# One lane of an attention stage moved one step back in the order that all engines follow

## The reference: what is computed

```python
h = L0_tok(x)                              # 8 x 748 tokens from here on
h = h + L0_attn(layernorm(h))              # a recurrence
h = h + L0_ffn(layernorm(h))               # 8 experts, top 2, and a shared part
h = h + L1_attn(layernorm(h))              # linear attention, below
h = h + L1_ffn(layernorm(h))               # router, 10 experts, shared 9-tap convolution

def L1_attn(x):                            # 8 heads of 16, causal
    q, k, v = split(x @ W_qkv + b_qkv)
    q, k = relu(q), relu(k)
    for w in (cos, sin):                   # position weights
        kv_cum = cumsum(outer(k * w, v));  k_cum = cumsum(k * w)
        ctx += (q * w) @ kv_cum;           nrm += (q * w) . k_cum
    return (ctx / (nrm + 1e-6)) @ W_out + b_out

def L1_ffn(x):
    logits = conv3(gelu(conv3(x, rc_w1)), rc_w2)          # router: 10 scores a token
    experts = top-2 mixture of elu(x @ e_w1) @ e_w2
    shared = conv1(silu(conv9(x, sh_w1)), sh_w2)          # 128 -> 512 -> 128
    return layernorm(x + experts + shared) * ln_g + ln_b
```

## Time and profile before

| | |
|---|---|
| median of 3 runs | 1550.25 us (1546.04 to 1556.02) |
| profiled execution, its own time | 1544.97 us |
| its span, first to last instruction | 1543.1 us |
| PE busy | 1312.4 us, 85% |
| DVE, POOL, ACT busy | 989.1, 698.2, 640.2 us |
| mean granted clock of TensorE | 0.917 |
| attention stage, from the first norm5T on PE to the last rc2 | about 565 to 1178 us |

### The profile page before, as it was taken

The page is one execution under the profiler, slowest core; times in us unless marked ns, Lnnn a source line. Parts: engine busy times, 40 slices in busy tenths (PEclk is TensorE's granted clock), DMA queues, the critical chain, the costliest instruction groups (busy, mean ns, idle before and its releaser), DMA issues.

```text
span 1543.1 us, 33563 instructions
## 1 busy us (share of the span) xinstructions
PE 1312.4 (85%) x10456; PEld 1129.8 (73%) x10457; DVE 989.1 (64%) x3229; ACT 640.2 (41%) x1594; POOL 698.2 (45%) x1055
## 2 busy tenths in 40 slices
PE   5687685976999927798999889988999989999974
PEld 3475654654999915596788778876888989999952
DVE  5386868664566547737762776357752729989956
ACT  2427355331222204245334533435434346666623
POOL 0123645435788833033612353232522536777732
PEclk9798887998999958979998999989998999999987
DMA  6000400003788730100110001000100237777725
GB/s 194 0 21 24 106 20 20 23 19 115 239 257 261 230 109 1 43 1 1 42 43 2 1 22 63 0 2 4 39 1 1 95 104 192 195 195 199 196 88 161
DMA packets 102203, 128.48 MB, mean 83 GB/s; under 512 B 21015, under 2 KB 61181, under 8 KB 101842
## 3 DMA queue, kind: packets, MB, share of 16 engines
q1 hardware_dynamic: 88786, 102.36, 23.0%
q0 software_dynamic: 13312, 24.74, 4.8%
HBM read 96.13 MB, written 34.94 MB: 85 GB/s over the span
## 4 chain that ended last, share of the span: by engine, by line
PE 60%; DVE 16%; issue 7%; DVEq 6%; POOL 4%; ACT 4%; DMA 2%; POOLq 0%; SPq 0%; ACTq 0%
PE psum L977 12%; PE psum L1123 10%; PE psum L986 9%; DVE work L1540 3%; PE psum L1044 3%; PE psum L1102 3%; POOL rows_in L2110 2%; PE psum L1132 2%; PE psum L791 2%; PE psum L1091 2%; PE psum L1069 2%; PE psum L1181 2%; PE psum L966 2%; DVE stats L1523 2%; PE psum L1015 2%
## 5 line engine op out<-in xcount | busy, mean ns | idle before, releaser
L1123 PE MATMUL psum<-NT,wreg 128*128 128x182 f32 (+1 forms) x1536 | 269.6, 333 | 5.2 <-ACT conv_rows L1434 4.3
L1123 PEld LDWEIGHTS psum<-NT,wreg 128*128 128x128 f32 x1536 | 256.2, 197 | 9.9 <-ACT conv_rows L1434 5.4
L2142 POOL DMA_INDIRECT rows_out<-work,expert_row_kept x208 | 206.6, 993 | 78.6 <-issue 40.9
L977 PE MATMUL psum<-work 128*128 128x128 f32 x1664 | 222.8, 277 | 0.9 <-ACT work L1326 0.9
L977 PEld LDWEIGHTS psum<-work 128*128 128x128 f32 x1664 | 204.1, 193 | 1.7 <-issue 0.9
L2091 POOL TENSOR_TENSOR rstd<-var_eps,pack 128x6 f32<-128x6 f32 x40 | 56.7, 1418 | 207.0 <-DVE var_eps L1530 206.7
L1319 ACT ACTIVATE work<-psum,work 128x128 f32<-128x128 f32 x416 | 118.9, 369 | 64.3 <-PE psum L977 64.3
L791 PE MATMUL psum<-pack,work 128*128 128x128 f32 (+2 forms) x288 | 54.0, 348 | 82.5 <-DVE work L1540 75.9
L1862 DVE SCALAR_TENSOR_TENSOR work<-psum,work 128x128 f32<-128x128 f32 x416 | 117.2, 344 | 7.8
L1871 DVE TENSOR_SCALAR work<-psum,expert_row_kept 128x128 f32<-128x128 f32 x208 | 72.8, 350 | 72.1 <-PE psum L966 37.3
L2110 POOL DMA_INDIRECT rows_in<-N,slot_now x96 | 100.6, 1048 | 28.5 <-issue 28.4
(11 more groups left out here) (357 smaller groups left out, 2910.2 us busy)
## 6 DMA issues: line engine op xcount, KB each, us to landing
work<-w_and_b SPq DMA_DIRECT2D x104, 258.0 KB
work<-in_ew SPq DMA_DIRECT2D x104, 256.0 KB
work<-rows_in SPq DMA_DIRECT2D x208, 65.0 KB
work<-rows_out SPq DMA_DIRECT2D x32, 384.0 KB, 4.5
rows_out<-work,expert_row_kept POOLq DMA_INDIRECT x208
work<-in_xT SPq DMA_DIRECT2D x8, 375.0 KB, 4.3
w_and_b<-in_ew SPq DMA_DIRECT2D x1, 2560.0 KB
out<-H SPq DMA_DIRECT2D x8, 320.0 KB
```

What stands on the lines that cost most here:

```text
L977: r_ = mm(v.ps1[:, c * P:(c + 1) * P], v.w1[:, c * P:(c + 1) * P], v.xT, start=True, stop=True)
L1123: r = mm(bank[:, half * HALF_PAIRS:half * HALF_PAIRS + p1 - p0], weights[:, m * P:(m + 1) * P], product_input(name, g, k, p0, p1), start=( ...
L2142: G.indirect_dma_start(rows_out[m], bass.IndirectOffsetOnAxis(ap=v.dest, axis=0), v.y, None, bounds_check=last, oob_is_err=False).then_inc ...
```

## The change

The pairs are now listed with lane 1 one step behind lane 0: step n of lane 0 is followed by step n-1 of lane 1. The list begins with steps 0 and 1 of lane 0 and ends with step 23 of lane 1. The weight of a step in `FILL` goes with the step, so the conv parts shift against the steps a little; the routing work stays tied to its (step, lane). POOL's and SP's lists are not touched.

The DVE work of steps 0 to 2 is handed out anew. Before, it ran as `h3`(0), `var5`(0), `h3`(1), `norm5`(0), `var5`(1), `norm5`(1) (lane in brackets); the new functions give the same row in the new order of steps, and only the convolution's work between them moves.

```diff
         def interleaved(conv):

             order, n, reached = [], 0, 0
-            for x in range(ATT_STEPS * LANES):
-                order.append(("attention", x // LANES, x % LANES))
-                reached += FILL[x // LANES]
+            for x in range((ATT_STEPS + LANES - 1) * LANES):
+                lane_ = x % LANES
+                step = x // LANES - lane_
+                if not 0 <= step < ATT_STEPS:
+                    continue
+                order.append(("attention", step, lane_))
+                reached += FILL[step]
                 while conv and n * sum(FILL) * LANES < reached * len(PARTS) and n < len(PARTS):
                     order.append(("conv", n, 0))
                     n += 1
...
             def begin_lane(k, i):
                 add_experts(k, i)
-                if k == 0:
-                    var5(k, i)
+                if k > 0:
+                    norm5(k - 1, i)
+                var5(k, i)

             def second_step(k, i):
-                (norm5 if k == 0 else var5)(k, i)
-
-            def third_step(k, i):
-                if k > 0:
+                if k == LANES - 1:
                     norm5(k, i)

-            att = {0: [begin_lane], 1: [second_step], 2: [third_step]}
+            att = {0: [begin_lane], 1: [second_step]}
```

## The result

The changed kernel takes 1580.74 us (median of 4 runs, 1574.50 to 1581.97) where the kernel before takes 1548.14 (4 runs, 1545.39 to 1556.02): a ratio of 1.0187, 95% interval 1.0151 to 1.0224. So it is slower by about 1.6%, 21 to 29 us by the ratios. (All ratios here are the recorded ones; the quotients of the medians are 1.0211 and 1.0146.) The profiled execution took 1579.63 us, 34.7 more than that of before.

The account below looks back on a forecast made before the run. PE (TensorE), busy 157.6 of 171.5 us in iteration 2, was taken to set the pace. Terms of 6.3 us an iteration, three times, gave +18.9 us on 1550.25: 1569 us, range 1546 to 1583.

Parts of the forecast that it names:

- norm6T of lane 0: Loop, behind lane 1's last context step: PE waits 3.4 us for DVE's late norm6, +3.2 us an iteration, bounds 2.5 and 4.
- The clock behind it: Behind that new hole TensorE runs 3.4 us at clock 0.50: +1.7 us an iteration, bounds 0 and 3.4.
- rc2 of lane 1: One conv part left between rc1 and rc2; ACT's table load and gelu end late: +0.4 us an iteration, bounds 0 and 0.5.
- Where the chunks begin: First chunks: POOL's `b_v` and `b_sh2` block DVE's first lane 0 state update for 5.9 us; +2.0 us an iteration.
- the wash rival: DVE slips between POOL's instructions and the new hole brings no low clock: 1549 to 1564 us, middle 1556; chance 0.31.
- Where an iteration begins: Iteration start: the hole moves from ahead of q0 to behind it; 0 us, bounds -2 and +1.3.
- rc2's low clock: Around both rc2, now further apart: the 13.7 us at clock 0.50 may break up; -1 us an iteration, bounds -3 and 0.
- The loop's sum: All terms of one loop iteration add to 6.3 us, three times: +18.9 us.
- Iteration 0: Iteration without convolution: gains a q step at its start, loses at its end behind norm6T; 0 us, bounds -4 and +4.
- Much slower: Rival: holes bring two low-clock stretches each and the iteration without convolution loses 4 us; 1583 us, chance 0.06.

Follow-up runs that it names:

- second comparison: The changed kernel measured and profiled again with no edit, against the kernel before: 1573.43 us, ratio 1.0135.
- lag_from_out: Changed kernel with lanes level up to the output projection, lane 1 one step behind only from there on, every iteration: 1566.72 us, ratio 1.0136 to the kernel before.
- level_from_out: Changed kernel with the lag ending at the output projection, lanes level from there on, every iteration: 1558.49 us, ratio 1.0071 to the kernel before.
- changed_mended: Changed kernel with DVE's norm6 of lane 0 ahead of lane 1's last context division, and POOL's conv weights early in iteration 0: ratio 0.9988 to before, on another chip.

## Why the prediction was right, and where it was not

Slower by 18.9 us was forecast; the medians differ by 32.6, and by 22.7 in the second comparison. The total, 1580.7 us, lies in the range of 1546 to 1583, near its end. The direction and the largest term came out by the mechanism that was given. That the total came out no further off is in part luck, since two errors have opposite signs: the loop was forecast 2 to 6 us too long, iteration 0 10 to 15 us too short.

**norm6T of lane 0, +3.2 us.** Right in size (3.65, 3.63 and 3.63 us in the three iterations, against 3.4) and in cause. In the loop the cause is shown three ways: the wait falls to 0.8 us when the context stands ahead of out (`lag_from_out`), and it is gone when the lag ends (`level_from_out`) and when, of the loop's work, DVE's norm6 alone is moved (`changed_mended`).

**The clock behind it, +1.7 us.** Right in place and about right in size. The three low stretches at this hole last 3.4, 6.8 and 3.4 us in the first profile and 6.8, 3.4 and 3.4 in the second. Less the 2.0 and 0.9 us of them that fall into the waits themselves, and halved for the clock, that is an estimated 1.9 to 2.1 us an iteration. They are there whenever the wait is and never without it. What varies between two executions is mostly the low clock elsewhere.

**rc2 of lane 1, +0.4 us.** 0.6 measured.

**Where the chunks begin, +2.0 us.** Wrong. The step that failed is that the first state update of lane 0 would stand still for 5.9 us beside `b_v` and `b_sh2`. It took 0.48 us, and the addition behind it 0.75 beside POOL's 2.24 (iteration 1):

```profile
740.90 0.48 DVE L1938 SCALAR_TENSOR_TENSOR first_row<-pack,psum,first_row 128x64 f32<-128x64 f32 x2
741.46 0.75 DVE L1941 TENSOR_TENSOR work<-work,upd 128x128 f32<-128x128 f32 x1
...
741.19 2.24 POOL L2167 TENSOR_TENSOR work<-work,row_bias 128x320 f32<-128x320 f32 x4 [4.87 <-ACT work L1358]
```

The first three instructions of the update were done or under way when POOL began; only the addition behind them met it, and it came in after the first of POOL's four, as the wash rival had it. That is also what the port rule of the Trainium skill ("SBUF — State Buffer", "Who interferes with whom") gives for this place; the 4.12 us of the earlier trace rows, five of POOL's instructions long, it doesn't give, and why the one place differs from the other no run shows. `b_sh2`, the larger part of the 5.9 us, then ran beside a mask, which took the same 1.23 us as elsewhere. The first chunks cost 4.6 us of holes in iteration 2 against 5.1 before: -0.4 instead of +2.0.

**Where an iteration begins, 0 us.** The hole moved as described, from norm5T of lane 1 to q1 of lane 0 behind ACT's relu. It measures 2.8, 3.4 and 3.4 us, where norm5T of lane 1 had 1.8, 3.5 and 3.0 in iterations 1 to 3. (The times that the prediction adds up for q1 give 871.9, not 870 to 871; with the 1.5 us that norm5 may come earlier they reach down to 870.4.)

**rc2's low clock, -1 us.** Not seen. The time at the low clock from rc1 to an iteration's end is 13.7 us in each iteration of before, 17.1, 20.5 and 17.1 in the first profile of the changed kernel and 13.7 each in the second. It was one stretch only in iteration 1 of before, the one of the earlier trace rows, and three in the others already; breaking up didn't make it shorter.

**The loop's sum.** Forecast 18.9 us; 16.7 in the first profile and 12.9 in the second. The holes are 11.4 and 10.5 us of it where the terms had 16.8: in the first profile the chunks' beginning is 7 us below its term over three iterations, and the other waits together are 2 us above theirs, the longer silu wait (0.4 each time) among them.

**Iteration 0, 0 us with -4 and +4 as bounds.** This is the term that was mis-sized: +14.6 us in the first profile, +9.6 in the second. The prediction named what happens at its end and set it off against the q step gained at the start. The holes say +7.7: the start gains 2.9 us, as meant, but the end loses 4.4 (two waits of 5.16 and 5.97 us for one of 6.74), the updates of the first two chunks lose 4.1 to three long POOL operations, and the other waits for updates and rc2 2.1 more. The clock adds 2.7 to 6.9. Iteration 0 has no conv parts, so nothing that the lag separates can be covered there; that was known from the earlier trace rows, and each of those waits could have been worked out from the rows as the loop's were. The three POOL operations of 3.4 us each that hold DVE there, for 10.1 us together, held it in the trace of before as well, for 6.4 us (the earlier trace rows shows one of them).

**The rivals.** The wash's condition on POOL and DVE came true in the loop, but its other half, a clock that stays up behind the hole, did not. (With that condition alone its sum is +1.3 us an iteration, where the prediction says +2.) "Much slower", at 1583 us, came nearest to the first measurement by its number, with iteration 0 losing more than its 4 us; of the double low stretches that it wanted behind each hole, one in three came.

## What to carry to other kernels

When one of two interleaved lanes is set back, list for every chain that had waited for both lanes at once what stands on each in-order engine between its start and its end: here one division of the other lane on DVE, waiting for a matmul that had just been set later, cost 3.6 us three times, and an estimated 2 us of clock with each. Moving that one instruction group on its own engine took the wait away without opening another; more filler ahead of the waiting matmuls took away about a third of the hole, and the clock lost that again. And cost the iteration that has no filler by itself, with the same care as the loop: it runs once, but it lost as much as two or three of the others.

## What the runs showed of the hardware

The changed kernel, in two executions, had some 135 and 112 us at the low clock in the four stretches (by their mean clocks, 0.77 and 0.82 in iteration 0), with holes equal to a microsecond in iteration 0 and in the loop. Where single profiles are compared at the level of 5 us, the holes say more than the lengths.

How long DVE stands still beside POOL is not one number. Two patterns are seen. In one each DVE instruction is held by one of POOL's: the norm that took 5.03 us instead of 1.63 has three instructions of 1.46 to 1.48 us, one beside each of POOL's of 1.44, and three of 0.34 behind them; in the loop an addition lost 0.5 us to the first of four short ones. In the other one DVE instruction is held by several of POOL's in a row: 4.12 us in the earlier trace rows, and 3.99 of the 4.63 us that an update took instead of 0.48, beside two short POOL instructions and one of 3.42. What decides between the two stays open:

```profile
595.02 4.63 DVE L1938 SCALAR_TENSOR_TENSOR first_row<-pack,psum,first_row 128x64 f32<-128x64 f32 x2
...
594.05 2.14 POOL L2167 TENSOR_TENSOR work<-work,row_bias 128x320 f32<-128x320 f32 x4 [2.00 <-ACT work L1358]
596.14 3.42 POOL L2191 TENSOR_TENSOR conv_h<-wreg 128x1536 f32<-128x1536 f32 x1
608.21 3.42 POOL L2193 TENSOR_TENSOR wreg<-conv_h,wreg 128x1536 f32<-128x1536 f32 x1 [8.64 <-issue]
```

The last row has an oddity of its own: 8.64 to 8.66 us of POOL pass ahead of the second operation on the weights in every kernel, wherever it stands: behind the first operation, behind `turn` and behind `b_out`. The kernel has an `e.drain()` ahead of both this operation and the third, and the third starts after 0.15 us, so a drain alone isn't it. DVE's operations in that time take their usual length (0.29 us for an addition), so POOL doesn't hold the port; the cause stays open.
